# The output projection of the second self attention as three f32r terms

## The reference

```python
attn = jax.nn.softmax(attn, axis=-1)
sa = jnp.einsum('bhts,bhsd->bhtd', attn, v).transpose(0, 2, 1, 3).reshape(B, T, C)
x = x + sa @ proj_w + proj_b
h = _layernorm(x, ln2_w, ln2_b)
```

## Time and profile before

| | us |
|---|---|
| three timed runs | 1782.29, 3129.28, 6248.3 |
| their median | 3129.28 |
| the profiled execution | 1786.37 |
| its span, first to last instruction | 1784.6 |
| mean granted TensorE clock, share of 2.4 GHz | 0.972 |

### The profile page before, as it was taken

The page is one execution under the profiler, slowest core; times in us unless marked ns, Lnnn a source line. Parts: engine busy times, 40 slices in busy tenths (PEclk is TensorE's granted clock), DMA queues, the critical chain, the costliest instruction groups (busy, mean ns, idle before and its releaser), DMA issues. The chain is left out here.

```text
span 1784.6 us, 28218 instructions
## 1 busy us (share of the span) xinstructions
PE 1621.7 (91%) x9620; PEld 1057.6 (59%) x9620; DVE 1136.5 (64%) x1976; ACT 1056.8 (59%) x1387; POOL 966.0 (54%) x737
## 2 busy tenths in 40 slices
PE   5889999999999999988998989996989888698799
PEld 3445545444444444378787978884544436477579
DVE  7567677777777777476775833447787855586513
ACT  4566688888888888833556433311676773354452
POOL 1466688888888888952233610202334444486405
PEclk9999999999999999999999999996999999899899
DMA  2011121111111111030000010103234321000101
GB/s 96 26 34 33 36 69 37 43 35 41 50 50 35 41 35 36 25 107 27 1 2 10 4 39 24 25 13 78 66 73 109 73 74 28 13 1 1 36 15 48
DMA packets 57109, 70.93 MB, mean 40 GB/s; under 512 B 21102, under 2 KB 44682, under 8 KB 57005
## 3 DMA queue, kind: packets, MB, share of 16 engines
q1 hardware_dynamic: 57005, 69.57, 13.9%
HBM read 41.59 MB, written 2.37 MB: 25 GB/s over the span
## 5 line engine op out<-in xcount | busy, mean ns | idle before, releaser
L1694 POOL TENSOR_TENSOR x<-x,sa_p_buf 128x1024 f32<-128x1024 f32 x190 | 453.3, 2386 | 125.6 <-ACT sa_p_buf L1430 112.9
L1562 DVE TENSOR_REDUCE sa_mx<-sa_front 128x1 f32<-128x512 f32 x512 | 327.7, 682 | 106.2 <-PE sa_front L1285 105.1
L1430 ACT ACTIVATE sa_p_buf<-sa_score 128x1024 f32<-128x1024 f32 x256 | 249.2, 1024 | 130.6 <-PE sa_score L1322 130.4
L1341 PE MATMUL sa_out<-sa_p_buf,sa_v_buf 128*64 128x512 f32 x1024 | 246.4, 602 | 0.0
L607 ACT ACTIVATE sa_p_buf<-sa_score 128x1024 f32<-128x1024 f32 (+1 forms) x160 | 140.5, 942 | 74.6 <-PE sa_score L555 74.5
L402 DVE TENSOR_REDUCE sa_mx<-sa_front 128x1 f32<-128x512 f32 (+1 forms) x224 | 136.5, 651 | 31.8 <-PE sa_front L316 28.3
L3067 POOL TENSOR_TENSOR x<-x,bias_out 128x1024 f32<-128x1024 f32 x24 | 59.6, 2498 | 172.7 <-POOLq L3395 142.0
L1341 PEld LDWEIGHTS sa_out<-sa_p_buf,sa_v_buf 128*64 128x64 f32 x1024 | 64.5, 136 | 123.5 <-issue 97.4
L1285 PE MATMUL sa_front<-sa_k_hi,sa_q_hi 64*128 64x512 f32 x512 | 117.1, 453 | 22.2 <-DVE sa_mx L1562 17.1
L1440 ACT ACTIVATE sa_score<-sa_m_all 128x1024 f32<-128x1024 f32 x128 | 130.9, 1035 | 0.4 <-DMA sa_m_all<-sa_m_line 0.4
L660 POOL TENSOR_SCALAR_AFFINE_SELECT sa_p_buf<-sa_p_buf 128x128 f32<-128x128 f32 x256 | 65.6, 293 | 119.2 <-ACT sa_p_buf L607 119.1
(11 more groups left out here) (290 smaller groups left out, 3541.2 us busy)
## 6 DMA issues: line engine op xcount, KB each, us to landing
sa_m_all<-sa_m_line SPq DMA_DIRECT2D x16, 512.0 KB, 3.6
x<-sa_m_line SPq DMA_DIRECT2D x16, 512.0 KB, 4.3
sa_v_buf<-o SPq DMA_DIRECT2D x15, 512.0 KB, 5.1
x<-in_x SPq DMA_DIRECT2D x8, 512.0 KB, 6.8
sa_q_stack<-sa_hi SPq DMA_DIRECT2D x32, 128.0 KB, 2.6
sa_k_stack<-sa_hi SPq DMA_DIRECT2D x32, 128.0 KB, 2.7
sa_recip<-sa_den_out SPq DMA_DIRECT2D x32, 128.0 KB, 2.7
ff_w<-in_L_xattn_ff_w SPq DMA_DIRECT2D x16, 128.0 KB, 2.2
```

Source lines behind the costliest of these rows:

```text
L1341: mm = pe.matmul(out_ps[64 * j:64 * j + 64, :], v_buf[:, b, kt, 64 * j:64 * j + 64], p_buf[:, s % NPB, j, :], start=(kt == 0), stop=(kt == ...
L1430: nc.scalar.activation(p_buf[:, s % NPB], score_ps[s % len(score_ps)][:], ACT.Exp, scale=SCALE).then_inc(exp_done, G)
L1562: dve.tensor_reduce(mx[:, b, j, qt, half:half + 1], front_ps[bank(item, j)][:], AX.X, ALU.max).then_inc(drained, 1)
L1694: nc.gpsimd.tensor_tensor(acc[:, h], prev, cur, ALU.add).then_inc(added, 1)
```

## The change

parts becomes a count of the slices of the source that are done in halves. The calls that had True get all their slices and are as before; po1 gets parts=NG, with NG = 4, all of its own. So tiles 2 to 15 of po1 are now done as three terms, with four buffers more in SBUF, and the weights are split once. ScalarE now also asks beside.source before it rounds a tile, which for tiles 8 to 15 is the wait for the scaling of the last quarter. The order of all hooks and lag=2 stay. The loop over slices from parts to KN is empty for every call, since parts equals KN.

```diff
     for k in range(parts, KN):
+        pe.matmul(dst, src[:, k, j * P:(j + 1) * P], wt[:, k, :], start=(k == parts), stop=False)
+    for k in range(parts):
+        pe.matmul(dst, s_hi[:, u, k, :], w_hi[:, k, :], start=(k == 0 and parts == KN), stop=False)
     if i == 1 and t == 0:
         pe.wait_ge(w_low.sem, w_low.since(1))
-    for k in range(KN):
+    for k in range(parts):
         pe.matmul(dst, s_hi[:, u, k, :], w_lo[:, k, :], start=False, stop=False)
     pe.wait_ge(src_low[j % 2].sem, src_low[j % 2].since((j - GROUP) // 2 + 1))
-    for k in range(KN):
-        mm = pe.matmul(dst, s_lo[:, u, k, :], w_hi[:, k, :], start=False, stop=(k == KN - 1))
+    for k in range(parts):
+        mm = pe.matmul(dst, s_lo[:, u, k, :], w_hi[:, k, :], start=False, stop=(k == parts - 1))
...
                 def high_parts(i):
                     for j in tiles_of(i):
                         at = slice(j * P, (j + 1) * P)
+                        beside.source(act, j)
                         if j >= RING + GROUP:
...
                 project_norm(nc, norm_sems, "po1", oT, wts, loads, True, x, True, hT, ident, None, fetch_kv,
-                             beside=finish(oT), lag=2)
+                             beside=finish(oT), parts=NG, lag=2)
```

More of the change, by code:

```diff
@@ L2972, in project_norm @@
 def project_norm(nc, shared, name, src, wts, loads, early, x, ln, hT, ident, out, prefetch=(), x_in=None, x_src=None,
-                 beside=Beside(), split=None, parts=False, lag=1):
+                 beside=Beside(), split=None, parts=0, lag=1):
     groups, at = [], 0
@@ L2997, in project_norm @@
         if parts:
-            w_hi, w_lo = [sb(n, [P, KN, D], F32R) for n in ("w_hi", "w_lo")]
-            s_hi, s_lo = [sb(n, [P, RING, KN, P], F32R) for n in ("src_hi", "src_lo")]
+            w_hi, w_lo = [sb(n, [P, parts, D], F32R) for n in ("w_hi", "w_lo")]
+            s_hi, s_lo = [sb(n, [P, RING, parts, P], F32R) for n in ("src_hi", "src_lo")]
         prod = [ctx.enter_context(nc.psum_tensor(f"{name}_prod{i}", [P, GROUP, D], F32)) for i in range(NPROD)]
@@ L3035, in low_part @@
             at = slice(j * P, (j + 1) * P)
-            engine.tensor_tensor(s_lo[:, j % RING], src[:, :, at], s_hi[:, j % RING].bitcast(F32),
+            engine.tensor_tensor(s_lo[:, j % RING], src[:, 0:parts, at], s_hi[:, j % RING].bitcast(F32),
                                  ALU.subtract).then_inc(src_low[j % 2].sem, 1)
@@ L3128, in product_of_parts @@
                     pe.wait_ge(src_high.sem, src_high.since(j - GROUP + 1))
-                    for k in range(KN):
-                        pe.matmul(dst, s_hi[:, u, k, :], w_hi[:, k, :], start=(k == 0), stop=False)
+                    for k in range(parts, KN):
+                        pe.matmul(dst, src[:, k, j * P:(j + 1) * P], wt[:, k, :], start=(k == parts), stop=False)
+                    for k in range(parts):
+                        pe.matmul(dst, s_hi[:, u, k, :], w_hi[:, k, :], start=(k == 0 and parts == KN), stop=False)
                     if i == 1 and t == 0:
                         pe.wait_ge(w_low.sem, w_low.since(1))
-                    for k in range(KN):
+                    for k in range(parts):
                         pe.matmul(dst, s_hi[:, u, k, :], w_lo[:, k, :], start=False, stop=False)
                     pe.wait_ge(src_low[j % 2].sem, src_low[j % 2].since((j - GROUP) // 2 + 1))
-                    for k in range(KN):
-                        mm = pe.matmul(dst, s_lo[:, u, k, :], w_hi[:, k, :], start=False, stop=(k == KN - 1))
+                    for k in range(parts):
+                        mm = pe.matmul(dst, s_lo[:, u, k, :], w_hi[:, k, :], start=False, stop=(k == parts - 1))
                     return mm
@@ L3215, in _ @@
                     dve.wait_ge(w_high.sem, w_high.since(1))
-                    dve.tensor_tensor(w_lo[:], wt[:], w_hi[:].bitcast(F32), ALU.subtract).then_inc(w_low.sem, 1)
+                    dve.tensor_tensor(w_lo[:], wt[:, 0:parts], w_hi[:].bitcast(F32), ALU.subtract).then_inc(w_low.sem, 1)
                     low_parts(1)
@@ L3263, in high_parts @@
                             act.wait_ge(prod_full.sem, prod_full.since(pe_at))
-                        nc.scalar.activation(s_hi[:, j % RING], src[:, :, at],
+                        nc.scalar.activation(s_hi[:, j % RING], src[:, 0:parts, at],
                                              ACT.Identity).then_inc(src_high.sem, 1)
@@ L3268, in _ @@
                     act.wait_ge(loaded.sem, loaded.since(DMA * len(loads)))
-                    nc.scalar.activation(w_hi[:], wt[:], ACT.Identity).then_inc(w_high.sem, 1)
+                    nc.scalar.activation(w_hi[:], wt[:, 0:parts], ACT.Identity).then_inc(w_high.sem, 1)
                     high_parts(1)
@@ L3528, in decoder_blocks @@
                     project_norm(nc, norm_sems, "po0", oT, wts, loads, True, x, True, hT, ident, None, fetch_kv, x_in, x_dram,
-                                 parts=True)
+                                 parts=NG)
                     loads = norm_loads(wts, [(w_out[:], by_rows(L0["ca_wo"]))], L0["ca_bo"], (L0["ln3_g"], L0["ln3_b"]))
@@ L3580, in decoder_blocks @@
             ff_ctx.close()
-            project_norm(nc, norm_sems, "pf1", hid, wts, loads, True, x, False, hT, ident, out_dram, parts=True)
+            project_norm(nc, norm_sems, "pf1", hid, wts, loads, True, x, False, hT, ident, out_dram, parts=4 * D // P)
 def causal_rows():
```

## The result

The changed kernel takes 1797.8 us (median of six executions, 1796.9 to 1799.2), the kernel before 1784.2, the median of six times of which two, 3129 and 6248 us, are long ones that did not come again. The other four lie between 1782.2 and 1785.0, with a median of 1782.9. The ratio without the long ones is given as 1.007, with a 95% interval from 1.006 to 1.008. The forecast was 1789 us, +4.6. The time lies inside the range, at its upper end, but the loss is about three times the one forecast.

What follows compares the result with a forecast made beforehand. TensorE's f32 products were taken to set po1's steady pace, 3.89 us a group. Terms of 2.2 (pace), 1 (opening), 1 (bias and scaling) and 0.4 (tail) gave +4.6 on 1784.3, so 1789 us, range 1779 to 1798.

Steps and rivals of the forecast that it cites:

- The pace: po1's time per group of two tiles: from 3.89 us to 4.74, or 5.35 with the variance step held by GpSimd.
- the step that decides: VectorE's order in po1 with lag=2: low half comes after statistics awaiting the product ahead, so TensorE waits 1.3 us.
- I take it that the old 4 us are gone: po1, products 1 to 6: old stall and low clock vanish, so 26.1 us against 23.4, a term of +2.2.
- upper bound of 4 us for bias and scaling: GpSimd's bias additions and scaling in po1 now stand between low halves and may hold VectorE: 0 to 4 us, taken +1.
- The opening and the tail: po1's head, low halves perhaps late behind GpSimd: 0 to 3 us, taken +1; its last 9.3 us, one low half: +0.4.
- The next stage moves by the whole sum: Behind po1: the next stage has its weights already, so its start shifts by the whole +4.6 us.
- the clock as a rival inside po1: TensorE, 62% busy in po1, drops to the lower clock in five groups: +14 us, 1798 us; chance 0.08.
- clock low into the next stage: Behind po1: the reason given for a result slower than the 2% band; chance 0.02.
- The gain arrives: po1: low halves ready in time, pace 3.3 to 3.5 us a group: -4 us, 1780 us; chance 0.12.
- The lock bites everywhere: po1: each of five groups meets one more GpSimd operation, opening costs 3 us: +10, 1794 us; chance 0.22.
- Nothing moves: po1: old stall was the larger part, pace loses only 0.85 us a group: 0 to +1.5, 1785 us; chance 0.13.

Runs made afterwards that it cites:

- e1: Changed kernel with VectorE making the low half two groups ahead before it waits for the next group's product: 1793.2 us, ratio 1.0034, stage 44.6 us.
- e7: Changed kernel with low halves first, po1's bias and last-quarter scaling cut to a few columns (computation left out): 1784.2 us, ratio 0.9994, stage 34.5.
- e8: Kernel before with po1's bias and last-quarter scaling cut to a few columns (computation left out): 1783.7 us, ratio 0.9995, stage 35.8.
- e9: Changed kernel with low halves first and the four bias additions moved into the attention ahead, on GpSimd: 1786.9 us, ratio 0.9998, stage 36.4.
- e10: Kernel before with the four bias additions moved into the attention ahead, on GpSimd: 1783.6 us, ratio 0.9992, stage 37.0.

## Why the prediction was right and wrong

**The pace: right.** The low half of the even tile behind a wait for the product ahead was the step that decides, and it is: 1.33 us of waiting inside each product of the steady pace (forecast 1.3), a period of 4.90 without the lock (4.74), 5.4 to 5.5 with a variance step held up (5.35). The last of these three is right in part by chance: in product 5 the variance step lost only 0.3 us, and the rest is the sum behind the normalisation that met add_bias(3). The times of the matmuls, of VectorE's low half (0.68 us) and of GpSimd's (1.27, forecast 1.33) were read from rows of other stages and hit. The order as such costs 3.4 us of the stage by e1.

**"I take it that the old 4 us are gone": wrong.** From the end of product 1 to that of product 6 it takes 30.6 us (1488.42 to 1519.06), not 26.1, against 23.4 before. The periods are 5.5, 9.35, 5.45, 5.4 and 4.9. Of the 4.5 us of the miss 4.0 are in the second. There the first normalisation stood for 4.63 us, TensorE 2.58 for it, and the clock fell behind that to the lower level for 6.8 us, as it did before the change at 1496 for 3.4. The old stall was not in the way of the new order; it came again, with 4.0 us against 3.9. The normalisation itself stood longer than before, 4.63 against 2.64, because add_bias(2) and the scaling now follow each other directly behind low halves, where before a wait for a DMA had parted them. The lock holds each of the two instructions of a normalisation once, so two operations of GpSimd in a row cost it both. I had that in the upper bound of 4 us for bias and scaling, and took 1: this is the term of the sum that was too small.

**The opening and the tail: right.** The end of product 1 lies 7.4 us behind the stage's start, against 7.0 before: +0.4, forecast +0.5 (1, less the 0.57 of the shorter product). From the end of product 6 to the next stage it takes 9.9 against 9.6, +0.3 for +0.4. Together with the 7.2 these are the 7.9 us.

**"The next stage moves by the whole sum": wrong.** The part behind took 5.1 us more. The forecast knew of the clock as a rival inside po1, of TensorE at 62%, and charged 9.6 us for it there. There it was at the lower level for 6.8 us behind the first stall, which can have cost 3.4 us at most. That stages of the same code could run at another clock was in no case but for half a sentence (the chance of 0.02 for "clock low into the next stage"). The runs showed two courses of the clock there, 261.1 to 262.1 us and 265.9 to 266.8; what picks one is open. The rival's total of 1798 is what was measured, but by another way: neither this rival nor that of the lock was right alone. So it is luck, too, that the time lies in the range: its upper end of 1798 was drawn for a low clock in five groups, which did not come.

**The rivals.** *The gain arrives*: not with this order, but e7 against e8 shows its condition met and 1.3 us of the stage won, not 4. *The lock bites everywhere*: it bit at the first and at the third normalisation and at five variance steps (0.43 to 0.79 us for 0.17), not in each. *Nothing moves*: no.

## What to carry to other kernels

Before a product is cut into cheaper terms, write down for the engine that makes the terms' inputs what it waits for directly ahead of them; with a deeper lag the helper's place in that engine's loop has to move too. Where GpSimd and VectorE both work on SBUF, look for each operation of GpSimd at what VectorE issues while it runs: it can hold one instruction, and two operations in a row held both of a normalisation. Long ones that need no partner (a bias) can go where nothing waits for them, as in e9 and e10. And this kernel has two times some 5 us apart, by the clock behind the changed stage, and a change of 2 us ahead of it switched profiled executions between them. So compare such variants stage by stage, with the clock of each.

## What the runs showed of the hardware

The clock's courses above: same code, same gaps, 126.5 to 127.2 us or 130.0 to 130.6 for the cross attention, and 1.9 us of idling after which the kernel was 2.8 and 2.4 us faster in two pairs and 0.1 us slower in the third, by the medians (the last two across sets). Further, VectorE's variance step, two elements a partition and 0.17 us when free, took up to 0.79 us in the changed kernel and 1.45 in the kernel before, so the size of the VectorE instruction is no protection. Not every VectorE instruction is held: while GpSimd made two low halves from 1488.40 to 1491.09, the sum that reads PSUM took its 0.69 us at 1488.53, and the statistics of two tiles 0.75 us at 1489.25. And GpSimd is held as well: its low half of 1.27 us took 2.29 at 1483.35, where VectorE made the weights' low half beside it.
